# Ten scatter pieces per attention batch instead of eight, and two per expert tile after that

## What is computed

```
xn  = layernorm(x)                               # [16, 512, 128]
q, k, v = heads(xn @ Wq), heads(xn @ Wk), heads(xn @ Wv)      # 16 heads of 8
sim = 8 * l2norm(q) @ l2norm(k).T                # causal
att = softmax(sim) @ v @ Wo
probs = softmax(xn @ Wr.T)                       # 8 experts
top_v, top_i = top_k(probs, 2); top_v /= sum(top_v)
for e in range(8):
    h = gelu(xn @ W1[e].T + b1[e])               # 512 hidden
    out += (h @ W2[e].T + b2[e]) * w_e           # w_e: top_v where top_i == e
return x + att + out
```

## Time and profile before

| | |
|---|---|
| median of 3 runs | 788.98 us (787.18 to 789.99) |
| the profiled execution | 787.53 us |
| its span, first to last instruction | 785.6 us |
| granted clock of TensorE, mean | 0.96 of full speed |
| PE, ACT, DVE, POOL busy | 87%, 61%, 67%, 56% |

### The profile page before, as it was taken

The page is one execution under the profiler, slowest core; times in us unless marked ns, Lnnn a source line. Parts: engine busy times, 40 slices in busy tenths (PEclk is TensorE's granted clock), DMA queues, the critical chain, the costliest instruction groups (busy, mean ns, idle before and its releaser), DMA issues. The chain is left out here.

```text
span 785.6 us, 19167 instructions
## 1 busy us (share of the span) xinstructions
PE 683.7 (87%) x5959; PEld 422.1 (54%) x5959; DVE 527.6 (67%) x1350; ACT 483.1 (61%) x801; POOL 443.2 (56%) x558
## 2 busy tenths in 40 slices
PE   2879297999999978988799997989898999999976
PEld 2757022333333338887799996878794333333322
DVE  7699985788888863333344444555554899999955
ACT  2777176888889853333344442334347898988983
POOL 4455346777777756655600035656604777787772
PEclk9999678999999999999999999999998999999997
DMA  6876555445433446434322233333322354554431
GB/s 197 265 249 204 139 165 111 102 96 106 98 86 82 101 134 181 147 107 121 93 81 67 71 86 97 94 93 101 97 58 59 79 116 108 118 116 92 93 97 34
DMA packets 170228, 89.18 MB, mean 114 GB/s; under 512 B 77216, under 2 KB 159936, under 8 KB 170176
## 3 DMA queue, kind: packets, MB, share of 16 engines
q1 hardware_dynamic: 161984, 71.74, 36.1%
q0 software_dynamic: 8192, 16.79, 7.5%
HBM read 39.47 MB, written 32.24 MB: 91 GB/s over the span
## 5 line engine op out<-in xcount | busy, mean ns | idle before, releaser
L701 ACT ACTIVATE prob<-psum 128x1024 f32<-128x1024 f32 x320 | 313.2, 1026 | 62.1 <-PE psum L793 49.0
L711 ACT ACTIVATE prob<-psum,prob 128x256 f32<-128x256 f32 x284 | 116.3, 471 | 190.2 <-PE psum L932 163.4
L818 PE MATMUL psum<-prob,v 128*18 128x384 f32 (+2 forms) x2560 | 180.1, 390 | 3.1 <-DVE prob L1205 1.7
L932 PE MATMUL psum<-xs,prob 128*128 128x256 f32 x568 | 139.3, 389 | 29.9 <-DVE xs L1335 21.7
L556 POOL DMA_INDIRECT slot_x<-rows,idx x128 | 129.3, 1010 | 57.1 <-issue 29.0
L554 POOL DMA_INDIRECT rows<-slot_y,idx x128 | 127.6, 997 | 57.1 <-issue 28.3
L567 POOL TENSOR_SCALAR_AFFINE_SELECT prob<-prob 128x512 f32<-128x512 f32 x128 | 89.9, 702 | 99.6 <-ACT prob L701 98.9
L793 PE MATMUL psum<-qks 32*128 32x512 f16 (+3 forms) x1024 | 127.7, 309 | 19.3 <-DMA qks<-dup 10.4
L944 PEld LDWEIGHTS psum<-prob 128*128 128x128 f32 x1136 | 138.1, 192 | 5.0 <-issue 1.2
L944 PE MATMUL psum<-prob 128*128 128x128 f32 x1136 | 138.4, 275 | 1.3 <-issue 1.3
L793 PEld LDWEIGHTS psum<-qks 32*128 32x128 f16 x1024 | 34.0, 92 | 181.9 <-ACT prob L701 95.0
(11 more groups left out here) (141 smaller groups left out, 678.3 us busy)
## 6 DMA issues: line engine op xcount, KB each, us to landing
xs<-slot_x SPq DMA_DIRECT2D x71, 128.0 KB
slot_y<-xs SPq DMA_DIRECT2D x71, 128.0 KB
xs<-in_L_attn_x SPq DMA_DIRECT2D x16, 256.0 KB, 3.5
prob<-in_L_ffn_W SPq DMA_DIRECT2D x16, 256.0 KB, 3.6
xn_rows<-xns SPq DMA_DIRECT2D x16, 256.0 KB, 4.0
xn_cols<-xts SPq DMA_DIRECT2D x16, 256.0 KB, 4.0
xt<-xn_cols SPq DMA_DIRECT2D x16, 256.0 KB
rows<-xn_rows SPq DMA_DIRECT2D x16, 256.0 KB
```

Of the source, the lines that this page charges most:

```text
L701: act.activation(prob[:, q % 2, KEPT[u], :], score[(q + u) % 2], ACT.Exp, scale=SCALE / UP ** 2).then_inc(exp_done, 1)
L711: act.activation(hs[:, s, c, :], psum[:, 2 * s + c // 2, (c % 2) * FT:(c % 2 + 1) * FT], ACT.Gelu, bias=ws[:, s, B1C + c:B1C + c + 1]).the ...
L818: mm = pe.matmul(ps_octet[w // 2][32 * g:32 * g + VW, first:first + cols], lhs, prob[:, w % 2, KEPT[u], c:c + cols], start=(i == 0 and not ...
L932: mm = pe.matmul(psum[:, 2 * s + c // 2, (c % 2) * FT:(c % 2 + 1) * FT], ws[:, s, c * P:(c + 1) * P], xgt[:, s, :], start=True, stop=True)
```

## The change

There are four edits.
- POOL, batches 1 to 7: ten pieces each instead of eight. The two more go in groups 1 and 3, between mask_first and the second mask_inner. The pieces are counted through (0 to 127), so a batch no longer sends its own eight: batch 1 sends pieces 8 to 17, and 78 are out after batch 7 instead of 64.
- POOL, experts: the other fifty go two per tile, one when the rows of the next tile are turned, one when W1's matmuls of this tile are done. The first four of them wait for no tile. The last one still goes in tile 22.
- SP: the row loads follow. In attention they stand in a table by batch and step (rows_at); in the experts they come every four tiles instead of every three.
- SP and POOL: the first eight batches are written out, without the loop. The other engines keep theirs.

```
+    MORE = MOVES + 2
+    SENT = MOVES + MORE * (HALF - 1)
+    LEAD = 4
...
+            rows_at = {(1, 1): 2, (2, 1): 3, (2, 4): 4, (3, 3): 5, (4, 2): 6, (5, 1): 7, (6, 1): 8, (6, 4): 9, (7, 3): 10}
...
                     for t in range(TB):
+                        if not second:
+                            rows_due(b, t)
                         if t == TB - 1 and not (known(b, HALF - 1) or known(b, NB - 2)):
                             load_xt(b + 2)
                         turn_qk(b + 1, t, 1 - par)
                 if not second:
-                    if not known(b, 0):
-                        load_rows(b + 1, 1 - par)
+                    rows_due(b, TB)
...
                 for k in range(3):
                     load_tile(k, k % 2)
-                load_rows(HALF + 1, 1)
...
-                    if isinstance(k, int) and k % 3 == 2 and HALF + 2 + k // 3 < NB:
-                        load_rows(HALF + 2 + k // 3, (HALF + 2 + k // 3) % 2)
+                    if known(k, 1):
+                        load_rows(HALF + 3, 1)
+                    if isinstance(k, int) and k % 4 == 0 and k > 0 and HALF + 3 + k // 4 < NB:
+                        load_rows(HALF + 3 + k // 4, (HALF + 3 + k // 4) % 2)
...
+            def send(b, w, place):
+                turn_of = [(w, place) for w in range(NQ) for place in ((0, 1, 2) if w % 2 else (0, 2))]
+                if (w, place) in turn_of:
+                    piece = MOVES + MORE * (b - 1) + turn_of.index((w, place))
+                    move(piece // MOVES, piece // MOVES % 2, piece % MOVES, False)
...
                             mask_first(n, w)
+                            if not second and not known(b, 0):
+                                send(b, w, 1)
                             mask_inner(n, w, 3)
...
-                for j in range(2):
-                    paced(HALF + j, j, 3 * j - 1, False)
-                with pool.Fori(HALF // 2 + 1, NB // 2) as i:
-                    for j in range(2):
-                        paced(2 * i + j, j, 6 * i + 3 * j - 3 * HALF - 1, False)
+                for piece in range(SENT, MOVES * NB):
+                    at_beat = piece - SENT - LEAD
+                    if some(at_beat + 1):
+                        at_tile(at_beat // 2, 2 * (at_beat % 2))
+                    move(piece // MOVES, piece // MOVES % 2, piece % MOVES, False)
```

More of the change, by code:

```diff
@@ L259, in stage_a, with attention @@
                 step(i, i % 2, i // 2)
-        def attention(eng, body, between):
-            for b in range(3):
+        def attention(eng, body, between, each=False):
+            for b in range(HALF if each else 3):
                 body(b, b % 2)
[L266 to L269, removed]
+            if not each:
+                with eng.Fori(1, HALF // 2 - 1) as i:
+                    body(2 * i + 1, 1)
+                    body(2 * i + 2, 0)
+                body(HALF - 1, 1)
             between()
@@ L397, in store_out, with rows_due @@
                 sp.dma_start(batch_rows(out, m), acc[:, at(TB * m, TB), :]).then_inc(stored, 16)
+            rows_at = {(1, 1): 2, (2, 1): 3, (2, 4): 4, (3, 3): 5, (4, 2): 6, (5, 1): 7, (6, 1): 8, (6, 4): 9, (7, 3): 10}
+            def rows_due(b, t):
+                if (b, t) in rows_at:
+                    load_rows(rows_at[b, t], rows_at[b, t] % 2)
             def body(b, par, second=False, last=False):
@@ L455, in between @@
                 store_tile(FFN_TILES - 1, (FFN_TILES - 1) % 2)
-            attention(sp, body, between)
+            attention(sp, body, between, each=True)
             sp.wait_ge(combined, MOVES * NB)
@@ L593, in body @@
                             pool.wait_ge(padded, 16 * E)
+                        if not second and not known(b, 0):
+                            send(b, w, 0 if half == 0 else 2)
+                            continue
                         order = [0], [1], [2], [3], [4], [5], [6], [7]
@@ L639, in between @@
                         paced(2 * i + j, j, 6 * i + 3 * j + RETURN0, True)
-            attention(pool, body, between)
+            attention(pool, body, between, each=True)
         @block.scalar
```

## The result

The changed kernel takes 784.95 us (median of 17 runs, 778.37 to 788.41), the kernel before 788.46 us beside it (17 runs, 785.03 to 793.09). The ratio is 0.994, with an interval of 0.992 to 0.997. That is 3.5 us between the medians and 4.6 us by the ratio, where 12.8 were forecast. The profiled execution took 783.66 us, its span 781.9 us, at a mean granted clock of 0.945 (0.960 before).

What follows compares the result with a forecast made beforehand. PE was taken as the bound, losing 17.8 us while pieces go out in the experts. Terms -14.3 + 0 + 1.5 = -12.8 us gave 774.7 for the profiled execution, 776 for the median; range 771 to 788.

Steps and rivals of the forecast that it cites:

- Experts, tiles 1 to 24: Sending stretch of the experts: spaced pieces no longer hold PE's results back; gain 14.3 us, bounds 4.1 and 17.8.
- seven copies of idx: Experts' sending stretch: loss expected to remain, 0.5 us for each idx copy that throws POOL behind, 3.5 us.
- At two per tile: Experts' sends: spacing becomes 1.87 us instead of 1.40, so POOL catches up two pieces after an idx copy.
- rival in which every piece costs the same: Experts' sends: cost per piece whatever the spacing; gain 4.1 us, attention takes 1.5, total 786; chance 0.10.
- Attention, batches 1 to 7: First attention half: two more pieces a batch make some POOL masks late; 1.5 us later, bounds -0.9 and +5.
- That fits, with 0.6 to spare.: POOL in attention: two more pieces cost 2.6 us a batch, against 3.2 us idle until an exponential.
- rival called overrun: Attention: pieces lengthened to 1.26 us overfill POOL's batches, 15 us eat the gain, about 789; chance 0.06.
- The bound: First attention half: at most +5 us, 0.35 us for each of 14 groups.
- untouched: Start of the experts: first W1 matmuls waited for DVE, whose chain stays unchanged; 0 us, bounds 0 and -1.
- Start of the experts: First tile load can go some 5 us sooner, but W1 matmuls waited for DVE: 0 us, bounds 0 and -1.
- End of sends, fetches, second half: After the sends: last piece still in tile 22, nothing queued on SP late, 0; fetching stretch unchanged at about 101 us.
- the second case: Experts' sends: every piece costs the same, whatever the spacing; gain 4.1 us, total 786; chance 0.10.

Runs made afterwards that it cites:

- e3_direct: The changed kernel with sends taking their indices from slots itself, without the copy of idx or the wait ahead of it: 779.84 us, ratio 0.986.
- e13_burst8: The changed kernel with its fifty expert pieces sent eight at once, every fourth tile: 804.10 us, 1.018 of the kernel before.
- e15_after: The changed kernel again, unaltered, on a chip of the first kind: 784.28 us, 0.994 of the kernel before.
- e2_twice: The kernel before with first attention half written out, and two pieces a batch sent again into an unread tensor: 797.14 us, ratio 1.010.
- e4_fetch2: The changed kernel with fetches paced two per tile instead of eight in three tiles: 767.71 us, 0.971 of the kernel before.
- e1_written: The kernel before with the first attention half written out on SyncE and GpSimd, nothing else changed: 788.21 us, ratio 0.997.
- e9_after: The changed kernel as it is, run again on a chip of the first kind: 786.14 us, 0.993 of the kernel before.
- e16_before: The kernel before itself, run again and profiled on a chip of the first kind: 787.65 us, ratio 0.999.
- e12_even: The changed kernel without idx copies in sends and expert-stage fetches, fetches two per tile, extra pieces behind groups 0 and 2's third mask: 763.24 us, ratio 0.965.
- e17_after: The changed kernel once more, unaltered, on a chip of the second kind: 757.28 us, 1.004 of the kernel before.

## Why the prediction was wrong

**Experts, tiles 1 to 24: right.** -14.3 forecast, -15.1 measured, PE busy 87.45 of 88.46 us. The mechanism was right in that unbroken runs hold results back. The 3.5 us that I left for seven copies of idx were not what stayed lost: e3_direct, without these copies, takes 83.8 us from tile 2 to 24 and the changed kernel 84.1 (83.9 and 84.2 in its other two profiles). "At two per tile" was not the point either: four in a run do nearly as well (86.2), eight undo the whole gain (104.9). That a run has to end before PE's slack does fits these two and the run of four at tile 5, which cost 1.2 us; the slack itself was not varied. The rival in which every piece costs the same is out, by e13_burst8 against e15_after.

**Attention, batches 1 to 7: the step that failed.** The term was +1.5 us, with an upper bound of +5. It was +10.7 up to W1's start (+7.1 in the six distances, +3.5 at the end of the half), by these parts of the argument:
- "That fits, with 0.6 to spare." POOL's need was summed with the durations of before. The masks grew from 697 to 762 ns, eight a batch, 0.5 us; the pieces from 1029 to 1045 ns, ten a batch, 0.2 us. The spare was gone: with these durations the need is 8.9 us of masks, 10 x 1.22 of pieces and 1.2 of copies of idx, 22.3 us, and the batches lasted 22.2 to 22.7. POOL was busy 19.9 us of a batch, 18.9 forecast. The rival called overrun was to decide from 1.05 us per piece on, and they took 1.045. So its mechanism came true, with a smaller price.
- The bound looked at PE's wait for masks alone: 3.0 us in the half, at the edge of what I had named. I left out DVE, whose steps beside a full POOL grew as well (its mask from 695 to 838 ns), and with it the last transpose of a batch, 0.54 us late. In its landing 0.54 became 1.86 us (e2_twice, e3_direct and e4_fetch2 show the wait in the same place, 2.0 to 2.1 us each). Why it grows is open: in these profiles the last part lands 2.0 to 2.1 us after the start of a code load, but in before and e1_written the code load also starts within 3.1 us of the transpose's issue, and nothing is lost, and in e9_after all sixteen parts are late.
- No term stood for the clock. After a wait of 2.06 us PE ran at half speed for some 6 us and the distance was 4.7 us longer; after one of 1.96 us in e9_after it did not, and it was 1.7 us longer.
- The end of the half, priced at nothing because DVE's chain was "untouched", gave 3.5 us. PE waited 0.41 and 1.79 us for POOL's masks behind pieces, and its last 24 matmuls took 1.2 us longer by the clock. Where the clock stayed up there (e9_after) the stretch was no shorter, 17.1 us, since the change's unpaced pieces ahead of the experts kept PE's result from DVE for 1.4 us: the mechanism that I had found for the experts, not counted here.

**Start of the experts: 0 forecast, +1.3 measured** (tile 0 to tile 2, 8.41 instead of 7.16 us). The clock makes the difference, but not surely the change: the kernel before took 8.61 us in e16_before, the changed one 7.70 in e9_after. **End of sends, fetches, second half: 0, right within 0.3 us** in this profile. It was not right in general: POOL's wait for rows led to the run at tile 5, and in the six other profiles of the first kind with the change's sends the fetches at the old pace took 121.4 to 125.6 us.

The sum by measured terms is -15.8 (tiles 2 to 24) + 10.7 + 1.3 + 0.1, which is -3.7 us, as the spans say. That the time fell into the range of 771 to 788 was luck: the range had been carried to the second case, in which every piece costs the same, and that case is ruled out.

**Left open.** Why PE's results are held on chips of the first kind and not on the second, and whether the kind is the chip's. What the hold is: the trace calls the wait by no name or by PE's. Why a transpose's parts land late. What lengthens the fetches behind the change's sends. Which part of e12_even's 22.4 us a batch is still POOL.

## What to carry to other kernels

When work is moved to an engine with idle time, sum its need with durations that the new overlap makes longer, and ask what the other engine beside it loses; then follow the latest thing each feeds, transposes as well as masks. Break runs of indirect DMAs every three or four pieces wherever PE's results have to reach others, the pieces ahead of a stage too, since a pause cost nothing here, and where the kernel takes 787 us or more its absence cost 15 to 20 us a stretch. And a gain that rests on a nameless wait should be measured on more than one chip, and at more than one time, before it is paid for elsewhere: here the price was paid on both kinds and the gain had on one.

## What the runs showed of the hardware

- In the series where the kernel before takes 787 to 792 us, an unbroken run of indirect DMAs, one each 1.26 us, keeps results of PE from the other engines from about its third or fourth piece until it ends (e13_burst8: copy at 346.55, last piece until 346.42). In those where it takes 755 to 756 us the same instructions at the same 1.25 us hold nothing (e17_after). Chip number 0 stands on the record with both.
- A wait of PE of about 2 us sometimes brings its clock to the lower level (0.61 us for matmuls of 0.39) and sometimes not. In the same place, waits of 2.06, 2.02 and 1.96 us were followed by a mean granted clock of 0.87, 0.93 and 1.00 and distances of 26.5, 24.9 and 23.4 us. Single runs of the changed kernel differ by 10 us; how much of it is this was not measured.
- With GpSimd full, its mask of 128x512 went from 697 to 762 ns and VectorE's from 695 to 838 ns.
- An indirect DMA can take its indices from a slice of a larger tile; leaving out the copy into idx was worth 3 to 6 us in all.
